# Weight preparation merged into the first half of a decoder-layer kernel: key weights and x first, the other weights split in the first score steps, bias rows picked by a selector

## What is computed

```python
# 1. relative-position self-attention over the 8 positions, 16 heads of 32, for each of 512 columns
q, k, v = split(x @ in_proj_weight.T + in_proj_bias)
p  = pos @ pos_proj_weight.T + pos_proj_bias
ac = einsum('tbhd,sbhd->bhts', q + r_w_bias, k)
bd = rel_shift(einsum('tbhd,rhd->bhtr', q + r_r_bias, p))
x1 = layernorm(x + softmax((ac + bd) / sqrt(32)) @ v @ out_proj_weight.T + out_proj_bias)
# 2. cross attention, 8 heads of 64, on a context (8, 512, 1024) with a key mask
kv = ctx @ W_src.T + b_src;  qx = x1 @ W_tgt.T + b_tgt
x2 = layernorm(x1 + cat(x1, attention(qx, kv)) @ W_out.T + b_out)
# 3. feed forward, hidden layer and second weight rounded to fp8, sums to fp16
h = relu(x2 @ w1.T + b1)
out = layernorm(x2 + round16(fp8(h) @ fp8(w2).T + round16(b2)))
```

## Time and profile before

| What | Value |
| --- | --- |
| median of 3 runs | 1962.86 us |
| the profiled execution | 1961.34 us, span 1959.5 us |
| TensorE granted clock, mean over the span | 0.982 of full |
| PE busy | 1845.5 us (94%) |
| DVE busy | 1333.6 us (68%) |
| ACT, POOL busy | 787.2 us (40%), 522.3 us (27%) |
| instructions | 33372 |

### The profile page before, as it was taken

One profiled execution on the slowest core, in us unless ns is written; L12 is line 12 of the kernel. 1 busy time (PEld: TensorE's weight loads), 2 busy tenths in 40 slices (PEclk: granted clock), 3 DMA queues, 4 the chain that ended last, 5 costly groups with the idle time before them and its releaser, 6 DMA issues. The chain is left out here.

```text
span 1959.5 us, 33372 instructions
## 1 busy us (share of the span) xinstructions
PE 1845.5 (94%) x12588; PEld 1016.1 (52%) x12588; DVE 1333.6 (68%) x1698; ACT 787.2 (40%) x1209; POOL 522.3 (27%) x546
## 2 busy tenths in 40 slices
PE   5999999999989999868999999999999999999988
PEld 4565555645544665445545455455454554544543
DVE  3588999899879989767565564655655556556521
ACT  3422222222222222247465363562653644626522
POOL 1334864585448326600000001001001000010010
PEclk8999999999999999989999999999999999999999
DMA  6545347425643456565313304104123041041000
GB/s 227 113 119 116 81 116 167 118 71 140 146 108 80 126 141 154 149 141 178 73 42 58 100 1 103 55 1 109 48 46 99 14 103 55 1 104 33 12 33 22
DMA packets 290831, 176.60 MB, mean 90 GB/s; under 512 B 194793, under 2 KB 248041, under 8 KB 290690
## 3 DMA queue, kind: packets, MB, share of 16 engines
q1 hardware_dynamic: 286320, 174.17, 35.6%
q10 hardware_dynamic: 4370, 0.34, 0.2%
HBM read 94.75 MB, written 33.55 MB: 65 GB/s over the span
## 5 line engine op out<-in xcount | busy, mean ns | idle before, releaser
L1362 DVE TENSOR_TENSOR p_lo<-k,p_hi 128x1024 f16<-128x1024 f32 x128 | 156.8, 1225 | 193.8 <-ACT p_hi L1250 193.8
L81 POOL TENSOR_TENSOR vsb<-mvb,consts 128x1 f32<-128x1 f32 x64 | 12.1, 189 | 1029.4 <-DVE mvb L1377 1029.4
L1051 PE MATMUL b_ff<-x2T_hi,w1T_hi 128*128 128x512 f16 x512 | 195.0, 381 | 2.3 <-DVE x2T_lo L1362 2.3
L1407 DVE CUSTOM_DVE_ANT_0 junk<-b_sx,mneg 128x512 f16<-128x512 f32 x256 | 176.1, 688 | 30.6 <-issue 22.2
L1051 PE MATMUL b_ff<-x2T_lo,w1T_hi 128*128 128x512 f16 x512 | 195.0, 381 | 0.0
L1051 PE MATMUL b_ff<-x2T_hi,w1T_lo 128*128 128x512 f16 x512 | 194.8, 380 | 0.0
L1282 ACT ACTIVATE k<-b_st,mbias 128x512 f32<-128x512 f32 x256 | 161.8, 685 | 14.1 <-PE b_st L1095 14.1
L1250 ACT ACTIVATE p_hi<-k 128x1024 f16<-128x1024 f32 x128 | 135.3, 1057 | 44.1 <-PE b_av L1110 41.7
L745 DVE TENSOR_TENSOR prod<-q,k 128x4096 f32<-128x4096 f32 x32 | 143.2, 4476 | 13.0 <-ACT q L677 12.1
L1274 ACT ACTIVATE hq<-b_ff,b 128x512 fp8e4<-128x512 f32 x128 | 88.0, 687 | 155.9 <-PE b_ff L1051 149.2
L595 PE MATMUL pj_b<-winT_hi,xT_hi 128*128 128x512 f16 x384 | 146.3, 381 | 3.9 <-DMA xT_lo<-rows_lo 3.9
(11 more groups left out here) (258 smaller groups left out, 4332.6 us busy)
## 6 DMA issues: line engine op xcount, KB each, us to landing
cn<-in_ctx_dram SPq DMA_DIRECT2D x64, 256.0 KB, 3.1
k<-kT_scratch SPq DMA_DIRECT2D x24, 512.0 KB, 7.8
xn<-in_x_dram SPq DMA_DIRECT2D x32, 256.0 KB, 3.0
x<-in_x_dram SPq DMA_DIRECT2D x32, 256.0 KB, 3.2
x_scratch<-x SPq DMA_DIRECT2D x32, 256.0 KB, 2.2
q<-x_scratch SPq DMA_DIRECT2D x8, 1024.0 KB, 5.6
q<-x_scratch SPq DMA_DIRECT2D x32, 256.0 KB, 4.1
out_dram<-q SPq DMA_DIRECT2D x32, 256.0 KB, 4.3
```

The source lines that it names most:

```text
L1051: mm = pe.matmul(out, a, c, start=(start and n == 0), stop=end)
L1362: dve.tensor_tensor(dst, bank, hi, ALU.subtract).then_inc(out, 1)
L1407: dve.tensor_tensor_reduce(junk[:, :], sx_b[tt % 2][:, :], mneg[:, :], 1.0, NEG, ALU.add, ALU.max, mx[:, h % 2, tt:tt + 1]).then_inc(s["sx ...
```

## The change

`prepare_a` and its barrier are gone. Its work is in phase A:

- SP's first load is row tile 0 of x, then the key third `wk` of the input projection (1 MB), then tile 1. The small loads are the same in kind (6 for biases, 2 for r_w, positions, 3 bias columns) and go first on ACT's queue. ACT also issues the other weights: `wq`, then `wp` during position 0 of the key loop, `wv` during position 2.
- There are 36 weight jobs in one order: 4 key, 4 query, 4 position, 4 value, 16 source, 4 output. They all use the three banks `sm_b`. The four key jobs stand before the key loop, a query or position job after each key projection, and the other 24 in score steps 0 to 3, six in each (`OPENING`, with `LOW_AFTER_PRODUCT` and `LOW_AFTER_SUM` for DVE).
- The last 20 jobs are fed by a ring of three 256 KB buffers (`load_ring`), which are the residual buffers `x1`: load r waits until job r-3 has been transposed.
- Quarters: block 0 has none in steps 2 and 3 now, and the last value steps take two more. x of block 1 is loaded and turned in steps 4 to 11 instead of 1 to 8.
- Bias: `raw` is 12 rows by 512 (high and low rows of six biases) instead of 2 by 3072, and the matmul that adds a bias multiplies `rows` by a selector `pick` which has ones in the two rows of that bias. It has the same shape as before.

```diff
-    SCORES_FIRST = (0, 0, 1, 1, 1, 1, 1, 1)
+    SCORES_FIRST = (0, 0, 0, 0, 1, 1, 1, 1)
     SCORES = (2, 1, 1, 2, 1, 1, 2, 1)
     VALUES = (2, 1, 1, 0, 0, 0, 0, 0)
-    VALUES_LAST = (2, 2, 2, 2, 2, 1, 1, 1)
+    VALUES_LAST = (2, 2, 2, 2, 2, 2, 2, 1)
+    OPENING = ((("w", 12), ("w", 13), ("w", 14), ("q", 1), ("pos", 0), ("w", 15), ("w", 16), ("w", 17)),
+               (("q", 2), ("g", 0), ("v", 0), ("w", 18), ("w", 19), ("w", 20), ("v", 1), ("w", 21), ("w", 22), ("w", 23)),
...
+               (("q", 7), ("v", 7)),
+               ())
+    LOW_AFTER_PRODUCT = ((12, 13, 14), (18, 19, 20), (24, 25, 26), (30, 31, 32))
+    LOW_AFTER_SUM = ((15, 16, 17), (21, 22, 23), (27, 28, 29), (33, 34, 35))
...
+            def load_ring(r):
+
+                if r >= 3:
+                    sp.wait_ge(s["wt_filled"], WSRC + r - 2)
...
+            load_rows("x", 0)
+            sp.dma_start(wk_n, d.in_w[E:2 * E, :].rearrange("(o p) k -> p o k", p=P)).then_inc(win_ld["wk"], 16)
+            load_rows("x", 1)
...
+            def weight_transposes(n):
...
                 if n >= 3:
-                    pe.wait_ge(ws_lo, n - 2)
+                    if WP <= n - 3 < WV:
+                        pe.wait_ge(s["wt_hi"], n - 2)
+                    else:
+                        pe.wait_ge(s["wt_lo"], lows_through(n - 3))
...
+            pe.wait_ge(s["made"], 2)
+            for n in range(WK, WQ):
+                weight_transposes(n)
+            position_transposes()
             for t in range(T):
-                weight_transposes(2 * t)
-                weight_transposes(2 * t + 1)
                 projection("k", t)
+                weight_transposes(WQ + t)
             projection("q", 0)
+            for g in range(8):
+                opening(g)
...
             firsts = list(plan.first_uses)
             for use in firsts[:3]:
                 row_hi(*use)
+            act.dma_start(wq_n, d.in_w[0:E, :].rearrange("(o p) k -> p o k", p=P)).then_inc(win_ld["wq"], 16)
+            for n in range(WK, WQ):
+                weights_hi(n)
...
+            for g in range(8):
+                score_products(0, g)
+                for n in plan.LOW_AFTER_PRODUCT[g] if g < 4 else ():
+                    weights_lo(n)
+                if g == 1:
+                    position_bias()
+                for n in plan.quarters(g - 1):
+                    stage_lo(n)
+                score_sums(0, g)
+                for n in plan.LOW_AFTER_SUM[g] if g < 4 else ():
+                    weights_lo(n)
+                if g == 0:
+                    positions()
+                if g == 2:
+                    position_weights()
```

More of the change, by code:

```diff
@@ new lines, in position_weights @@
+            def position_weights():
+                for e in range(KT):
+                    if e == 2:
+                        pe.wait_ge(s["step"], 6)
+                    for o in range(4):
+                        mm = pe.matmul(gb[e // 2][:, (e % 2) * 256 + o * 64:(e % 2) * 256 + (o + 1) * 64],
+                                       wq_n[:, o, e * P:(e + 1) * P], pb[:, o, :, :].rearrange("p h r -> p (h r)"),
+                                       start=True, stop=True)
+                    if e % 2:
+                        mm.then_inc(s["g_filled"], 1)
@@ L587, in projection @@
                     a = "qkv".index(kind)
-                    rhs = [z[:, :, a * E:(a + 1) * E] for z in w.winT]
-                    bias, out = w.rows[:, a * E:(a + 1) * E], pj_b[n % 3][:, :]
+                    rhs = [z[:, :, a * E:(a + 1) * E] for z in winT]
+                    ones, bias, out = pick[:, BIAS[kind], :], rows[:, :], pj_b[n % 3][:, :]
+                if i == 0:
+                    if kind == "p":
+                        pe.wait_ge(s["g_lo"], 2)
+                        pe.wait_ge(s["step"], 8)
+                    else:
+                        pe.wait_ge(s["wt_lo"], lows_through({"k": WK, "q": WQ, "v": WV}[kind] + 3))
                 wait_turned(pe, "x", i)
@@ L595, in projection @@
                         pe.matmul(out, a, c, start=(j == 0 and m == 0), stop=False)
-                pe.matmul(out, w.ones[:, 0:P], bias, start=False, stop=True).then_inc(s["pj_filled"], 1)
+                if (kind, i) == ("k", 0):
+                    pe.wait_ge(s["step"], 5)
+                pe.matmul(out, ones, bias, start=False, stop=True).then_inc(s["pj_filled"], 1)
             def output_projection(n):
+                if n == 0:
+                    pe.wait_ge(s["wt_lo"], lows_through(WEND - 1))
                 wait_turned(pe, "o", n)
@@ L603, in output_projection @@
                 for j in range(KT):
-                    for m, (a, c) in enumerate(terms([z[:, j, :] for z in c1T], [z[:, j, :] for z in w.woT])):
+                    for m, (a, c) in enumerate(terms([z[:, j, :] for z in c1T], [z[:, j, :] for z in woT])):
                         pe.matmul(out, a, c, start=(j == 0 and m == 0), stop=False)
-                pe.matmul(out, w.ones[:, 0:P], w.rows[:, BO:BS], start=False, stop=True).then_inc(s["om_filled"], 1)
+                pe.matmul(out, pick[:, BIAS["out"], :], rows[:, :], start=False, stop=True).then_inc(s["om_filled"], 1)
             def context_products(n):
@@ L815, in _ @@
+            for g in range(8, plan.STEPS):
                 b, t = g // 16, g % 8
```

491 lines of the change are left out of this document (250 added, 241 removed), and 5 rows, old and new, of the table OPENING.

## The result

The changed kernel is **slower by 0.3%**: 1968.72 us (median of 20 runs, 1961.89 to 1973.48) against 1962.61 us for the kernel before (20 runs beside it), ratio 1.0031, 95% interval 1.002 to 1.0043. Its profiled execution took 1965.41 us. The forecast was 1952.7 (1944.5 to 1961.0).

A forecast was written before the change was run, and what follows sets the result against it. It took phase A's chain to run through DVE, with PE close behind. -30.4 + 12 + 2.1 + 0.5 + 5.6 = -10.2 from 1961.34 gave 1951.1, plus 1.5 for the median: 1952.7 us, range 1944.5 to 1961.

The forecast's parts named there:

- term 1: Start of the scores: DVE's first product comes at 51.3 instead of 81.7, -30.4 us.
- term 2: Score steps of block 0: weight work now under them lengthens the eight steps from 81.2 to 93.2, +12 us.
- term 4: Last value steps: two more quarters make steps 14 and 15 go at PE's pace, +5.6 us.
- Blocks 1 to 2 keep their times: After block 0: PE is back in step before that block ends, so these blocks add no time.
- signs of being right: First key projection at 18 to 22, first product 49 to 54, softmax 142 to 149, block 1 near 242, output waits 2 to 3.
- The start S: Start of the first key projection in the changed kernel: taken as 20, bounds 16 and 25.
- rival 2: Key loop: rows of x wait behind weight loads, the scores start 5 later, 1957.7 us; chance 0.17.
- Term 3: Softmax of block 0: the 2.30 wait for the exponential grows by 2.1 because PE runs behind DVE.
- +0.5 for the wait for output projection 1: Value steps of block 0: DVE's wait of 1.90 for this projection grows by 0.5 us.
- rival 3: Score steps of block 0: slow landing of ring weight loads stalls DVE, up to 1979 us; chance 0.05.
- Rival 1: Last value steps: the end costs only the two low parts, 1.4, giving 1948.5 us; chance 0.13.
- The check by PE alone: Second sum, from PE's earlier start (-27.6) and added jobs and position products: -10.5 if its idle time stays.

The follow-up runs named there:

- run 3: Changed kernel with the quarter tables of the kernel before (block 0 has its two quarters again): 1962.46 us, ratio 1.0015 to the kernel before.
- Run 5: Changed kernel with the exponential ahead of the rows on ACT in step 8 of block 0 only: 1963.88 us, ratio 1.0015 to the kernel before.
- Run 2: Kernel before with only block 1's rows of x moved from steps 1 to 8 to steps 4 to 11: 1962.56 us, ratio 1.0013.
- runs 3 and 4: run 3, and the changed kernel with block 1's x rows two per step in steps 4 to 7: 1974.26 us, ratio 1.0074 to before.
- run 1: Kernel before with only the change's two quarter tables (the new tables): 1973.09 us, ratio 1.0069.
- 6 to 9: Exponential first in all blocks: changed kernel, new tables 1.0012, old tables 0.9956; kernel before, old tables 0.9956, new tables 1.0028.
- run 9: Kernel before with the change's quarter tables and the exponential first in all blocks: 1968.67 us, ratio 1.0028.

## Why the prediction was wrong, step by step

The prediction gave -10.2 and the trace shows +4.1. The misses, by its own terms: term 1 +3.3, term 2 +0.6, softmax 0 +5.2 (7.3 for 2.1), value steps of block 0 +1.3 (1.8 for 0.5), blocks 1 to 3 up to the last value steps +6.2 for nothing, term 4 -2.2. Two steps failed: the size and the cause of the wait in softmax 0, and "Blocks 1 to 2 keep their times". Of its signs of being right, the first projection (19.2) and the softmax (148.5) came true; the first product (54.7) missed by 0.7, block 1 (251.9 for 242) and the output waits of 2 to 3 us did not.

**Term 1** (-30.4) measured -27.1. The start S was right, 19.24 for 20. The key loop, with q and its copy, took 35.4 us for 31.3. PE's timeline, and ACT's for the row that PE waited for:

```profile
19.24 0.61 PE L537 MATMUL pj_b<-winT_hi,xT_hi 128*128 128x512 f16 x1 [0.88 <-DVE winT_lo L836]
19.64 0.63 PE L537 MATMUL pj_b<-winT_lo,xT_hi 128*128 128x512 f16 x1
24.76 0.85 PE L478 MATMUL sm_b<-ident,v 128*128 128x128 f32 x4
25.67 0.38 PE L537 MATMUL pj_b<-winT_lo,xT_hi 128*128 128x512 f16 x1
40.95 0.39 PE L537 MATMUL pj_b<-winT_hi,xT_hi 128*128 128x512 f16 x1 [2.37 <-DMA xT_lo<-rows_lo]
```

```profile
32.14 0.39 ACTq L733 DMA_DIRECT2D v<-in_in_w_dram  x1
37.57 0.63 ACT L631 ACTIVATE rows_hi<-xn 128x512 f16<-128x512 f32 x1 [4.79 <-DMA xn<-in_x_dram]
```

The first projection took 5.5 (24.76 - 19.24) for 4.65: its 13 passes start 0.43 us apart, those from 25.45 on 0.22 apart. So the half pace that the prediction expected came, and lasted for the whole projection; the granted clock reads 1.00 in this stretch all the same, so in this place it does not show the pace. PE also waited 2.37 for a row of x whose load was issued at 32.0, beside the 1 MB of value weights at 32.1 and 256 KB of source weights at 32.6, and was there at 37.6, where the median of a row is 3.0. Row 3 was as slow, 6.0 us from its issue at 15.0 beside the 1 MB of query weights, but PE did not need it yet. That is rival 2 at a small size: the row was late by about the margin and 2.4 us more. The rule of the Trainium skill cited for it (DMA: Bandwidth & Descriptors, Issuing engines are not separate DMA queues) fits both rows. The remaining 0.9 us of the key loop is spread over it.

**Term 2** (+12) measured +12.6. That the sum came out is partly luck: DVE had some 2.6 us less work than the 92.2 that was summed, and waited 4.2 where 1 was allowed. 3.2 of that is one wait for the high part of a value weight in step 0, which stood on ACT behind a row of context whose load was late (61.19). The base was read wrongly too: the chain of the score steps before did not run through DVE. PE was busy for all of their 81.2 us, and DVE waited for q in steps 5, 6 and 7 (2.30, 2.50, 2.52), of which the prediction named one. And the term is right for four quarters only. With six (run 3) the same steps take 104.3, PE busy for 99.5 of them and DVE for 90.7: the prediction summed PE's list to 90 and never asked what the two quarters' absence was worth, so it did not see that some 10 us of the gain at softmax 0 come from the tables, not from the merge.

**Term 3** is the first failed step. "The 2.30 wait grows by +2.1": it grew by 6.8. The prediction looked at PE's lateness; the wait came from rows ahead of the exponential on ACT, behind a queue of turns and loads on SP. Run 5 shows it: with the exponential first it is 0.46. Run 2 shows that the moved x is not enough to cause it: SP has to be late as well. It was late in runs 3 and 4 too, in which the steps are longer or the rows stand elsewhere; common to them is the order of ACT's list shown above, which no run undoes. Short steps by themselves do little: in run 1, with the old order, the score steps take 74.7 us and the wait is 3.94. The +0.5 for the wait for output projection 1 did not come either: it fell from 1.90 to 0.70.

**"PE is back in step before the block ends ... Blocks 1 to 2 keep their times"** is the second, and the larger miss. Before those blocks, the value steps of block 0 took 1.8 us more. DVE's two half sums, which take 2.26 and 1.22 alone, were held by the moved rows' low parts on POOL. POOL, then DVE:

```profile
192.96 1.16 POOL L434 TENSOR_TENSOR rows_lo<-xn,rows_hi 128x512 f16<-128x512 f32 x1
194.07 3.21 POOL L434 TENSOR_TENSOR rows_lo<-cn,rows_hi 128x512 f16<-128x512 f32 x1
```

```profile
193.94 2.33 DVE L814 TENSOR_TENSOR prod<-prod 128x2048 f32<-128x2048 f32 x1
196.30 2.06 DVE L816 TENSOR_TENSOR prod<-prod 128x1024 f32<-128x1024 f32 x1
```

The second sum takes 2.06 instead of 1.22, twice in block 0 (+1.7); run 2 has the same two 2.06 and value steps longer by 1.5. In blocks 1 to 3 the tables decide. A group of four quarters needs four context rows; the last is handled in the step of the quarter two ahead of the group's first, and turned one step later. If the group's first quarter is in the very step of the turn, PE can be kept waiting for it. Counted from the tables, old ones make this happen at three starts in blocks 1 and 2, all in score steps of block 1; new ones at four, in softmax step 8 of block 1 and steps 3, 6 and 9 of block 2, and at all six of block 3 (old: three). The traces have their large waits there: changed kernel 5.56 at 353.65 (step 8) and 6.40 at 490.30 (step 3); and runs 1, 3, 6 to 9 move with the tables, not with the merge: with the exponential first the new tables bring 15.9 us more of these waits and a last residual 11.1 later in the changed kernel, 15.3 more and 15.9 later in the kernel before. The count says where a wait can come, not that it does: no large wait stands at steps 6 and 9 of block 2, and one of 2.31 (320.62) stands at a start that it calls free.

**Term 4** (+5.6) measured +3.4 in the changed kernel, +4.4 in run 1 (109.6 for 105.2) and +4.9 in run 9 (108.5 for 103.6). The two quarters do cost time at the end, but not in the way forecast: the waits for output projections there are 1.3 to 1.5 us each before the last one, not 2 to 3, and in sum 11.4 where they were 11.6. What grew is DVE's own busy time, by 3.9: the two low parts (1.4), and four second sums at 2.06 beside POOL instead of two.

**Rivals.** The slower end was given to rival 3, a ring that starves the score steps. There was one wait for a ring weight's high part of 0.27 us in steps 1 to 3, so that one is refuted. Rival 1 said that the two low parts are all that the end costs; they are 1.4 of its 3.4 us. The mechanism that did make it slower, the tables' shift, was on the prediction's table as "quarters: none in steps 2 and 3 now", and it was costed at its place and at the end, never in between. **The check by PE alone** (-10.5 "if its idle time stays") rested on the condition that failed: the idle time for turned context alone grew by 11.0.

**The account** of the changed kernel in its one trace: -27.1 (start) +12.6 (score steps) +7.3 (softmax 0) +1.8 (value steps 0) +4.9 (block 1 to its first value product, 3.65 of it softmax) +1.3 (to block 3's) +3.4 (end) = +4.2, 4.1 by the marks; the medians say 6.1.

**Open**: why the 0.7% that the tables cost in the kernel before shows as only 0.16% (to within about 0.2%) between the changed kernel and run 3, where both have a long wait for the exponential, 9.11 and 7.31; and whether the merge can be made to gain by a better order of ACT's rows in block 0's score steps or of SP's queue, neither of which was tried.

## What to carry to other kernels

When a change moves pieces of a counted sequence (here quarters in groups of four) from one block to a later one, every block between gets another phase: list where each group starts against where its inputs are made ready, before and after, in all blocks. Undo such a table alone and try it alone before judging the rest of a change; here it cost 0.56 to 0.72% in three pairs of kernels and 0.16%, not clear of noise, in the fourth, and a merge that was neutral by itself came out slower with it. And ask, for each in-order queue, what stands ahead of the one instruction that the critical engine waits for: moving the exponential ahead of three row copies was worth 0.44% in the kernel before and 0.6% in the changed one with old tables.

## What the runs showed of the hardware

A GpSimd subtraction of 128x512 with two inputs in SBUF takes 1.16 us alone. Started while DVE runs a two-input sum in SBUF, it takes 3.21 (the fence above), and 5.29 when it starts 0.15 us into a 4.42 product of the scores (138.43); each of them ends some 1.0 us after the DVE instruction. The DVE sum issued behind such a sum then takes 0.84 longer (2.06 for 1.22). So neither looks slowed in proportion: each waits for the other to finish. The Trainium skill, SBUF — State Buffer, section SBUF: two separate sides, says that of two such instructions the one that starts second is blocked until the first is done; these rows agree. One fits less plainly: 5.75 us for a subtraction recorded as starting at 110.28, 0.33 before the product that it ends behind.

A long wait of PE costs more than its length. Its group of 128x256 passes after the 6.40 wait, and the wait itself (busy us of PE, PEld, DVE, ACT, POOL; PEclk, DMA share, GB/s):

```profile
483.90:490.30 6.40, 0.00 (x1) 0.03 (x1) 5.62 (x2) 1.38 (x3) 2.06 (x2) 0.67 0.82 235
490.30:494.40 4.10, 4.10 (x20) 2.84 (x21) 0.75 (x1) 1.09 (x2) 2.64 (x3) 0.50 0.43 102
```

The granted clock fell during the wait and stood at 0.50 behind it. The 28 passes from 490.30 to 496.23 start 0.21 us apart, the later ones 0.11, so the wait cost an estimated 2.9 us (28 x 0.104) on top of its 6.40.
